# One core, two convolution stages around an MLP: setup order, early loads, squares on another engine, and filler passes on TensorE

## What is computed

```python
y = conv_general_dilated(x, dw_w, padding=((3, 3), (3, 3)), feature_group_count=96) + dw_b   # 7x7, per channel
y = transpose(y, (0, 2, 3, 1))
mu, var = mean(y, -1), mean(square(y - mu), -1)
y = (y - mu) * rsqrt(var + 1e-6) * ln_w + ln_b
y = gelu(einsum('bhwc,cd->bhwd', y, w1) + b1)              # 96 -> 384
gx = sqrt(sum(square(y), axis=(1, 2)))                     # per image and hidden channel
nx = gx / (mean(gx, -1) + 1e-6)
y = grn_gamma * (y * nx) + grn_beta + y
y = einsum('bhwd,dc->bhwc', y, w2) + b2                    # 384 -> 96
x = x + transpose(y, (0, 3, 1, 2))
xq = clip(floor(x / 2**-16) * 2**-16, -32768, 32767)
w = sign(w) * exp2(round(log2(abs(clampabs(w, 2**-14, 1.0)))))
out = conv_general_dilated(xq, w, padding=((1, 1), (1, 1)), feature_group_count=96) + bq
```

## Time and profile before

| | us |
|---|---|
| median of 3 runs | 1080.11 |
| lowest and highest | 1079.97, 1080.11 |
| the profiled execution | 1080.37 |
| its span, first to last instruction | 1078.6 |
| PE busy in the span | 990.8 (92%) |
| ACT, DVE, POOL busy | 830.8, 825.5, 411.7 |
| granted TensorE clock, mean | 0.963 |

### The profile page before, as it was taken

One profiled execution on the slowest core, in us unless ns is written; L12 is line 12 of the kernel. 1 busy time (PEld: TensorE's weight loads), 2 busy tenths in 40 slices (PEclk: granted clock), 3 DMA queues, 4 the chain that ended last, 5 costly groups with the idle time before them and its releaser, 6 DMA issues.

```text
span 1078.6 us, 21092 instructions
## 1 busy us (share of the span) xinstructions
PE 990.8 (92%) x5574; PEld 717.7 (67%) x5574; DVE 825.5 (77%) x1768; ACT 830.8 (77%) x1724; POOL 411.7 (38%) x353
## 2 busy tenths in 40 slices
PE   3999999999999467999999999999999849999996
PEld 2788888888888355666666666666666427767774
DVE  7777777777777565888888888888887667888885
ACT  2688888888887357898988888888888607787874
POOL 2666676666666153332333333333332001111110
PEclk9999999999999766999999999999999978999999
DMA  8777777777772592555555555555543247999995
GB/s 162 147 183 182 181 179 184 187 187 179 180 179 66 131 225 82 157 175 163 172 162 171 172 162 170 162 171 162 167 136 90 80 110 187 245 248 243 247 244 154
DMA packets 146312, 182.95 MB, mean 170 GB/s; under 512 B 13799, under 2 KB 140424, under 8 KB 143208
## 3 DMA queue, kind: packets, MB, share of 16 engines
q1 hardware_dynamic: 145480, 179.97, 62.5%
q10 hardware_dynamic: 800, 2.61, 1.0%
HBM read 124.28 MB, written 58.25 MB: 169 GB/s over the span
## 4 chain that ended last, share of the span: by engine, by line
PE 71%; DVE 12%; ACT 6%; issue 6%; DMA 3%; DVEq 1%; POOL 0%; ACTq 0%; SPq 0%; POOLq 0%
PE psum L573 22%; PE psum L653 21%; PE psum L643 6%; PE psum L644 6%; PE psum L645 6%; PE psum L552 6%; PE psum L600 3%; DVE arena_r L894 3%; ACT arena L706 2%; ACT arena_r L691 2%; DVE arena L919 1%; DMA arena<-lines_a 1%; DVE arena L923 1%; DVE arena L1079 1%; DVE arena L1068 1%
## 5 line engine op out<-in xcount | busy, mean ns | idle before, releaser
L573 PE MATMUL psum<-arena_r 112*128 112x464 f32 x1536 | 375.2, 386 | 0.3 <-issue 0.2
L573 PEld LDWEIGHTS psum<-arena_r 112*128 112x128 f32 x1536 | 276.8, 190 | 33.9 <-issue 1.1
L653 PE MATMUL psum<-arena,w2s 128*96 128x448 f32 x672 | 266.8, 542 | 2.8 <-DVE w2s L994 2.8
L787 ACT ACTIVATE arena<-psum,b1g 128x448 f32<-128x448 f32 x336 | 201.8, 630 | 58.3 <-PE psum L645 58.2
L497 POOL TENSOR_TENSOR arena_r<-arena,arena_r 96x448 fp32r<-96x448 f32 x112 | 134.1, 1197 | 268.7 <-DVE arena_r L969 194.8
L653 PEld LDWEIGHTS psum<-arena,w2s 128*96 128x96 f32 x672 | 109.8, 164 | 119.1 <-issue 111.8
L643 PE MATMUL psum<-arena_r,w1h 96*128 96x448 f32 x336 | 154.1, 459 | 14.2 <-POOL arena_r L497 13.0
L706 ACT ACTIVATE arena<-psum,bias_a 64x224 f32<-64x224 f32 (+1 forms) x288 | 117.0, 442 | 61.8 <-PE psum L573 50.6
L894 DVE TENSOR_TENSOR arena_r<-psum,arena_r 112x224 fp32r<-112x224 f32 x384 | 127.2, 382 | 48.3 <-ACT arena_r L691 47.5
L691 ACT ACTIVATE arena_r<-psum 112x224 fp32r<-112x224 f32 x384 | 112.6, 355 | 54.8 <-PE psum L552 52.5
L486 POOL TENSOR_TENSOR arena<-arena 128x448 f32<-128x448 f32 x96 | 110.0, 1146 | 109.8 <-DVE arena L923 109.2
(11 more groups left out here) (94 smaller groups left out, 1146.1 us busy)
## 6 DMA issues: line engine op xcount, KB each, us to landing
arena<-lines_a SPq DMA_DIRECT2D x48, 448.0 KB
arena<-in_x_dram SPq DMA_DIRECT2D x48, 392.0 KB
y_scratch<-arena SPq DMA_DIRECT2D x48, 392.0 KB
arena<-in_x_dram SPq DMA_DIRECT2D x112, 168.0 KB, 2.5
z_scratch<-arena SPq DMA_DIRECT2D x112, 168.0 KB, 2.0
arena<-z_scratch SPq DMA_DIRECT2D x48, 392.0 KB
out_dram<-arena SPq DMA_DIRECT2D x48, 392.0 KB
arena_r<-y_scratch SPq DMA_DIRECT2D x98, 168.0 KB, 2.6
```

The lines of the kernel that those rows point to most:

```text
L573: mm = nc.tensor.matmul(p_conv[s % 2][:, 0:NCOL], w[:, p, s, TW * k:TW * k + TW], v[:, p, s, slot0 + k:slot0 + k + JP, :].rearrange("p j i ...
L653: mm = nc.tensor.matmul(p_o[k][0:C, 0:CH], w2s[:, p, m, :], hid[:, p, m, CH * t:CH * t + CH], start=(m == 0), stop=(m == MT - 1))
L787: nc.scalar.activation(hid[:, p, m, CH * t:CH * t + CH], p_h[m][:, 0:CH], ACT.Gelu, bias=b1g[:, m:m + 1]).then_inc(gelu_done, 1)
```

## The change

- `keep_warm` is new: PE runs a number of passes of 384 columns with w1h, whose result nobody reads: 50 after stage a's last transposes, 58 after the statistics are turned, 25 in stage c before the third group of its first batch.
- Setup: SP issues half of batch 0's rows, the lines as soon as they are made (one copy instead of 49), the other half, batch 0's tables in eight transfers of one channel each half, then batch 1's rows and tables, and last w1 and w2. The nine other small loads are on ACT's queue. DVE makes the lines first and stage c's weights and biases before its first low part. In batch 0 the next batch's groups are turned one channel later (`AHEAD0`). The convolution of stage a waits for the table halves per channel, not per batch.
- The back transposes and those of the statistics take 56 rows and 56 columns instead of 64, and `forwards` reads them with that step.
- Squares: for image 0 DVE does the three over chunks 0 to 3 and one of the other three; for the last image one. In image 1 the GRN product stands after the second up chunk and the first down after the fourth (`FIRST_LEAD`).
- Seam 2: `hid` of even images moves to the place of stage c's input, and the rows of images 0 to 13 and the tables of stage c's batches 0 and 1 are loaded once the down products of image 14 are done. Only images 14 and 15 are loaded after the last z. POOL clears the halos. Stage c's tables are loaded one batch ahead; stage a's stores lag by 2 batches instead of 3.

```diff
+AHEAD0 = ((), (0, 1), (2,), (3,))
...
 LEAD = 2
+WARM = (50, 58, 25)
+FIRST_LEAD = 3
...
-    return bass.AP(tensor=v.tensor, offset=v.offset + LSTEP - 1,
-                   ap=[part, [LSTEP, n], [bank, 2], [-1, W]])
+    return bass.AP(tensor=v.tensor, offset=v.offset + W - 1,
+                   ap=[part, [W, n], [bank, 2], [-1, W]])
...
+        hid0 = mlp(128, MT, HW)
         ct = mlp(C, 2, CH)
         xr = mlp(C, HW)
-        hid = mlp(128, 2, MT, HW)
...
+        hid = [hid0, mlp(128, MT, HW)]
+        sqv = mlp(128, SQ_WIDE)
...
+        NSMALL = 8
+
+        def by_vector(i, m, part):
+            return isinstance(i, int) and (i == 0 and (part == 0 or m == 0) or i == NIMG - 1 and part == 1 and m == 0)
+
+        V_FIRST, V_LAST = MT + 1, 1
...
-            load_rows(stages["a"], x_v, 0, 0)
-            for dst, src in ((wc, cw.rearrange("c o h w -> c (o h w)")),
...
-                sp.dma_start(dst, src, allow_slow_non_contiguous=True).then_inc(small_in, 16)
+
+            def half_rows(g):
+                sp.dma_start(xin[CR * g:CR * g + CR, 0, :, :],
+                             x_v.rearrange("(i g) c (m t) -> g (c m) i t", g=2, t=RUN)[g][0:CR]).then_inc(stages["a"]["x0"], 16)
+
+            half_rows(0)
...
             sp.wait_ge(lines_made, 1)
             store_lines(lines_a, la, zrow, KA)
+            half_rows(1)
             sp.wait_ge(lines_out, 3 * 16)
...
-                    shifted = bass.AP(tensor=lines, offset=b * (CB * kt * TW) + LPAD + r * LSTEP - (LSTEP - 1),
+                    shifted = bass.AP(tensor=lines, offset=b * (CB * kt * TW) + LPAD + r * LSTEP - (W - 1),
...
-                        if not (last and s == 1):
+                        if not (last and s == 1) and not (isinstance(b, int) and b == 0):
                             need(sp, S["tin"], G * b)
                             load_rows(S, src, b + 1, 1 - s)
-                            if ahead:
-                                tables(b + 1, 1 - s)
-                        if not ahead:
-                            tables(b, s)
-                        if not (isinstance(b, int) and b < 3):
-                            store(b - 3, 1 - s)
+                            tables(b + 1, 1 - s)
+                        if not (isinstance(b, int) and b < lag):
+                            store(b - lag, (s + lag) % 2)
                 bodies(sp, body, 2)
...
-            tables_a(0, 0)
-            conv_transfers(stages["a"], x_v, y_v, tables_a, True)
+            for k in range(CB):
+                for r in range(2):
+                    shifted = bass.AP(tensor=lines_a, offset=k * (KA * TW) + LPAD + r * LSTEP - (W - 1), ap=[[1, W], [1, KA * TW]])
+                    sp.dma_start(toep[W * r:W * r + W, 0, k, :], shifted).then_inc(t_first[k], 16)
+            load_rows(stages["a"], x_v, 1, 1)
+            tables_a(1, 1)
+            for dst, src in ((w1r, w1),
+                             (w2r[:, :, :], w2.rearrange("(t p) c -> p t c", p=128))):
+                sp.dma_start(dst, src).then_inc(small_in, 16)
+            conv_transfers(stages["a"], x_v, y_v, tables_a, 2)
...
+            def first_rows(b, i0, i1, done):
+
+                rows_of = z_v.rearrange("(i g) c (m t) -> g (c m) i t", g=2, t=RUN)
+                for g in range(2):
+                    sp.dma_start(xin[CR * g:CR * g + CR, b, i0:i1, :], rows_of[g][CR * b:CR * b + CR][:, i0:i1]).then_inc(done, 16)
+
+            sp.wait_ge(o_done, NCH * (NIMG - 1))
+            for k in range(4):
+                sp.wait_ge(z_out[k], 16 * Z_USES[k % 2] * (NIMG // 2 - 1))
+            for b in range(2):
+                first_rows(b, 0, NI2 - 1, c_early[b])
+                tables_c(b, b)
             step(NIMG, 0, more_y=False, more_x=False)
             for k in range(4):
                 sp.wait_ge(z_out[k], 16 * Z_USES[k % 2] * NIMG // 2)
-            load_rows(stages["c"], z_v, 0, 0)
-            sp.wait_ge(halo, 2)
-            conv_transfers(stages["c"], z_v, out_v, tables_c, False)
+            for b in range(2):
+                first_rows(b, NI2 - 1, NI2, stages["c"][f"x{b}"])
+            conv_transfers(stages["c"], z_v, out_v, tables_c, 3)
             for s in range(2):
...
-                    if t == NCH - 1 and not (fixed and i == NIMG):
+                    if t == (2 if fixed and i == 0 else NCH - 1) and not (fixed and i == NIMG):
 
                         pool.wait_ge(ss_ready, i + 1)
                         pool.tensor_tensor(gx[:, :], ss3[:, :], halves[:, :], ALU.pow).then_inc(gx_ready, 1)
...
+            pool.wait_ge(h_done, MT * NCH * NIMG)
+            for v in (xt_h, xt_l):
+                for slots in (slice(0, HALO), slice(HALO + NPAIR, SLOTS)):
+                    pool.memset(v[:, :, :, slots, :].bitcast(F32), 0.0).then_inc(halo, 1)
...
+            def keep_warm(passes, to=7):
+
+                for _ in range(passes):
+                    nc.tensor.matmul(bank[to][:, 0:HID], w1h[:, 0:128], w1h[:, :], start=True, stop=True)
...
+                    if S is stages["c"] and isinstance(b, int) and b < 2:
+                        if s == 0:
+                            pe.wait_ge(c_early[b], 32)
+                        if s == G - 1:
+                            pe.wait_ge(S[f"x{b}"], 32)
+                    elif s == 0:
                         pe.wait_ge(S[f"x{p}"], 16 * (b - p) + 32)
                     need(pe, S["xt"], n - 1)
...
+                    if S is stages["a"]:
+                        pe.wait_ge(S["th"], n + 1)
+                    channel = n
                     if s == 0:
-                        if S is stages["a"]:
-                            pe.wait_ge(S["tl"], CB * b + CB)
-                        else:
+                        if S is stages["c"]:
                             pe.wait_ge(S["th"], b + 1)
                         pe.wait_ge(S["xt"], G * b + G)
...
+                        if w is toep_l and k == 0:
+                            pe.wait_ge(S["tl"], channel + 1)
                         mm = nc.tensor.matmul(p_conv[s % 2][:, 0:NCOL], w[:, p, s, TW * k:TW * k + TW],
...
-                            mm = nc.tensor.transpose(outs[s % len(outs)][0:CM, 1 - r, LSTEP * n:LSTEP * n + LSTEP],
-                                                     yt[q:q + LSTEP, p, i, (h + 1 - r) % 2].rearrange("p g m -> p (g m)"),
-                                                     ident[q:q + LSTEP, q:q + LSTEP])
+                            mm = nc.tensor.transpose(outs[s % len(outs)][0:CM, 1 - r, W * n:W * n + W],
+                                                     yt[q:q + W, p, i, (h + 1 - r) % 2].rearrange("p g m -> p (g m)"),
+                                                     ident[q:q + W, q:q + W])
...
                 for s in range(G):
+                    if S is stages["c"] and s == 2:
+                        pe.wait_ge(gelu_done, MT * NCH * NIMG)
+                        keep_warm(WARM[2], 2)
                     tin(0, s, 0)
...
+            keep_warm(WARM[0])
             pe.wait_ge(stages["a"]["out"], C)
             pe.wait_ge(stat_in, 1)
...
+            keep_warm(WARM[1])
...
+                lead = FIRST_LEAD if fixed and i == 1 else LEAD
+                for t in range(NCH + lead):
                     if t < NCH and not tail:
                         up(i, p, t)
-                    if t == 0 and not head:
+                    if t == (1 if fixed and i == 1 else 0) and not head:
 
                         pe.wait_ge(gx_ready, i)
                         need(pe, v_ready, NCH * (i - 1) - 1)
                         nc.tensor.matmul(p_grn[1 - p], ones[:, :], gx[:, :], start=True, stop=True).then_inc(gsum_done, 1)
-                    if t >= LEAD and not head:
-                        down(i - 1, 1 - p, t - LEAD)
+                    if t >= lead and not head:
+                        down(i - 1, 1 - p, t - lead)
...
-            act.wait_ge(small_in, 16 * NSMALL)
+            for dst, src, done in ((wc, cw.rearrange("c o h w -> c (o h w)"), c_in),
+                                   (bq[0], cb.rearrange("(o c) -> o c", o=1).to_broadcast([TW, C]), c_in),
+                                   (bias_a[:, :], dw_b.rearrange("(o c) -> o c", o=1).to_broadcast([TW, C]), bias_in),
+                                   (b1t[:, :], b1.rearrange("(t p) -> p t", p=128), small_in),
+                                   (gam[:, :], grn_gamma.rearrange("(t p) -> p t", p=128), small_in),
+                                   (bet[:, :], grn_beta.rearrange("(t p) -> p t", p=128), small_in),
+                                   (lnw[:, :], ln_w.rearrange("(p o) -> p o", o=1), small_in),
+                                   (lnb[:, :], ln_b.rearrange("(p o) -> p o", o=1), small_in),
+                                   (b2c[:, :], b2.rearrange("(p o) -> p o", o=1), small_in)):
+                act.dma_start(dst, src, allow_slow_non_contiguous=True).then_inc(done, 16)
+            act.wait_ge(prep, 3)
```

(55 more changed lines are left out.)

127 lines of the change are left out of this document (55 added, 72 removed).

## The result

| | us |
|---|---|
| before, median of 4 runs | 1080.11 |
| after, median of 4 runs | 1070.74 (1069.77 to 1072.06) |
| ratio | 0.9907, 95% interval 0.9894 to 0.9919 |
| profiled span, before and after | 1078.6 and 1070.3 |

The change makes the kernel 9.4 us faster; forecast were 23.6. The 8.3 us between the two profiled spans, by where the same instruction of PE starts in both timelines: 6.1 are there when batch 2 of stage a begins its first convolution (49.24 against 55.30), 1.3 come between the last convolution of stage a and the first down product of image 1, 0.5 between that of image 15 and the first convolution of stage c's batch 2, 0.3 in the rest of stage c. Forecast for the two seams: 5.0 and 8.0. A stretch of one kernel varies from profile to profile (see the table of experiments), and of the kernel before there is only one.

The account below looks back on a forecast made before the run. PE bounds the steady loops, chains of DMA, DVE and ACT the seams. 1080.4 - 7.0 - 3.6 - 5.0 - 8.0 = 1056.8, less 0.3: 1056.5 us; range 1046 to 1069, chance of the forecast itself 0.52.

Parts of the forecast that it names:

- The start: Setup and stage a's first batches: earlier lines, tables and rows start the convolutions sooner; gain 7.0 us, bounds 3 and 10.
- The transposes: Back transposes of 56 instead of 64, at 0.84 ns a column, save 27 ns a group; gain 3.6 us, bounds 0 and 8.9.
- The new waits: Stage a's convolutions wait for their own channel's table halves, hidden because the semaphore is long set; 0, bounds 0 and -2.
- Seam 1: Stage a to the first down product: 5.5 to 8.3 us won, 1.2 to 3.1 lost; net gain 5.0, bounds -1 and 8.
- The passes: Unread passes between stage a and MLP: the 50 end 1.2 to 3.1 us late, 2.0 taken; the 58 cost nothing.
- The squares' step: Image 0's squares shared by DVE and ACT bring the GRN factor product at 408.9 against 414.34.
- 415.2 with the clock up, 418 with it down: When image 1's four chunks are up before the first down product, set against 423.5 before; 5.5 to 8.3 us won.
- Seam 2: MLP to stage c: early rows and tables leave two images per batch to load; gain 8.0 us, bounds 5.5 and 10.
- The z stores that wait behind them are due at 861.72, so nothing is late: End of MLP: eight early load issues from near 858, 3.7 us on SP's queue, don't delay the stores of z.
- its first batch is then set by ACT and the new order ahead, 7.9 us: Stage c's start: first convolution at 883.8, 7.8 us earlier; batch 1 at 891.7, 7.4 earlier.
- The passes stay at half clock: Rival: the unread passes don't lift PE's clock, ending 6.9 and 7.3 us late; seam between stage a and MLP -9; chance 0.08.
- Load-bound transposes: Rival: loading the unchanged 112 stationary columns sets the back transposes, so the 3.6 us are not there; 1060.1 us, chance 0.18.

Follow-up runs that it names:

- wide_64: The changed kernel with the transposes back on 64 rows and 64 moving columns, as in the kernel before: 1070.3 us.
- load_56: The changed kernel with stage a's transposes back loading 56 stationary columns instead of 112, output not the reference's; executed once, group of eight 0.31 us.
- c_order: The changed kernel with stage c's first batch in the order of the kernel before, stage a keeping the new order: 1069.2 us.

## Why the prediction was wrong

*The start (7.0, measured 6.1).* The steps held: tables issued from 7.41, first convolution at 15.57 (forecast 15.5 to 16). Batch 1 began at 33.98 against 32: the bias products waited for DVE (0.96 us) and came late themselves. Its first 12 passes ran mostly at half clock (4.33 us instead of 2.77), and batch 2 began at 49.24. A gain of 0.9 less, no wrong step.

*The transposes (3.6, measured 1 at most).* The group went from 0.367 to 0.357 us, 10 ns and not 27. The median period of stage a is 0.02 us shorter (13.90 to 13.88), that of c 0.02 (7.46 to 7.44), over 22 batches each some 0.8. In the profiled run a single batch of 14.41 us takes stage a's share back, so it isn't among the 8.3, and wide_64 shows nothing of it in the time. The failed step is the column cost taken from eight 112-column transposes and laid on pairs that were argued, not seen. The rule of the Trainium skill (TensorE: Matmul & The Clock Gate, "LDWEIGHTS"), a load that takes its columns at 1.2 GHz, gives by an estimate 0.75 us for 8 x 112 columns, 0.37 if they go in pairs, and no gain from the cut. The prediction took the trace to lean against that rule, and this reading was wrong: 0.367 us for four pairs is 92 ns a pair. The load time of 112 columns by the rule of the Trainium skill is 93 ns, an estimate, so the 64-column group didn't speak against it. The gain was indeed near that rival's. But by the same rule load_56 would come to 0.19, and it stayed at 0.31: the rule alone doesn't carry the group either, and what the fixed part is stays open.

*The new waits (0).* As forecast, 12 passes still take 2.77 us.

*Seam 1 (5.0, measured 1.3 in the profiled run, -0.6 to 0.9 in the other four with this seam).* The passes were right: they ended at 370.5, 3.1 us late, the end of the range, and the 58 cost nothing: they ran on to the first up product at 381.04, 1.3 us past its ready low half, and the wait before the next chunk (1.08 us for POOL) took that up. Of the 3.1 only 0.6 reached DVE's first scaling, since the store took 2.47 us and not the 4.55 of before, a gain that the sum did not have. The squares' step failed in three terms; all times here are counted from the end of stage a and put on the clock of before, 6.1 later. (1) The engines were priced alone: POOL's low halves beside DVE's squares took 2.85 and 2.37 instead of 1.15 to 1.47, and one of the squares took 2.76 instead of 2.0 (last section). The product's input was ready at 411.4, not 408.9. (2) I put the product where its input is ready, but it stands behind chunk 1 of image 1, which waited for POOL (5.36 us) and ran at half clock: 413.8. (3) The range "415.2 with the clock up, 418 with it down" was set against 423.5, the end of the fourth chunk before; but there the first down product stood ahead of that chunk, at 421.65. Now it began at 422.0, 0.3 after that of before, with one chunk more already up. Behind it VectorE still has chunks of image 1 to normalise. B comes out 1.3 shorter where 5.0 was forecast.

*Seam 2 (8.0, measured 0.5 in the profiled run, near 2 in most).* "The z stores that wait behind them are due at 861.72, so nothing is late" is the first step that failed. The queue itself was priced about right: the first store of image 15 is issued 7.46 us after the first down product, against 6.85 before. What was put at nothing is how long that store then takes beside the loads. The first row is of the chain that ended last, the other two are busy time by stretch, after and before:
```profile
854.87 7.45 DMA z_scratch<-arena
...
852.00:858.00 6.00, 6.00 (x16) 2.54 (x15) 5.21 (x9) 0.67 (x1) 0.00 (x0) 0.88 0.94 220
...
852.00:858.00 6.00, 3.22 (x6) 1.38 (x7) 5.01 (x14) 2.04 (x4) 0.00 (x0) 0.77 0.19 57
```
It lands after 7.45 us instead of 1.96, with the DMA engines 94% busy, and chunk 2's rounding needs its slot: DVE waits 2.78 us, and from there all stores come 3.8 us later than before, counted from the first down product. The half clock in the first down products lies behind this wait. In the eleven profiles with the loads on SP the wait ends 14.6 to 15.5 us after the first down product, whether PE took 11.5 or 14.5 us for its first 30 matmuls, and it is 2.8 to 5.7 us long. Counted from image 15's first down product the first convolution came 3.6 us later than forecast. The second is "its first batch is then set by ACT and the new order ahead, 7.9 us": with nothing of batch 1 transposed ahead, PE waits for DVE's low parts (1.23 us at 889.19), partly at half clock; two batches took 18.3 us where the forecast has 14.4. 3.6 and 3.9 are the 7.5 that are missing. 1.4 of the 3.9 are the half clock from 891.0, which eight of the eleven profiles with this order don't have; c_order has 14.8 for the two batches. That the 25 passes cost nothing was right; they also bought nothing, for the clock fell after the 3.12 us between them and x.

*The rivals.* "The passes stay at half clock", 1070.5, gives the measured time but by another way: a mean of 0.71 over their 12 us leaves 7 at half clock, then they ran at full. "Load-bound transposes" was near in its term. The case that was missing is this: at each seam the gain of one chain ends at the next wait on the same seam. It had no chance of its own beside the 0.52 for everything adding up, and the range ended at 1069, 1.7 short.
